# Attention rows: the copy of the attended values moves ahead of the second image's bias on VectorE

## What is computed

```python
x = x + _L0_conv_ref(_gn(x), ...)   # outlook attention: 3 x 3 patches weighted by a softmax over 9, 6 heads
x = x + _L1_conv_ref(_gn(x), ...)   # shifted-window attention: 7 x 7 windows, 12 heads of 16 channels
```

```python
attn = jnp.einsum('wmqd,wmkd->wmqk', q * hd ** (-0.5), k) + rpb[None]   # scores and relative bias
...
attn = jax.nn.softmax(attn.reshape(b * nW, NH, n, n), axis=-1)          # after the shift mask
out = jnp.einsum('wmqk,wmkd->wqmd', attn, v).reshape(b * nW, n, c)      # attended values
out = out @ proj_weight.T + proj_bias
```

## Time and profile before

| what | before |
|---|---|
| median of 3 runs | 3550.34 us (3539.38 to 3553.98) |
| profiled execution, own time | 3556.17 us |
| its span | 3554.1 us |
| TensorE busy (matmul) | 3286.0 us, 92% |
| VectorE busy | 2765.8 us, 78% |
| GpSimd busy | 2298.7 us, 65% |
| ScalarE busy | 1837.5 us, 52% |
| mean granted clock of TensorE | 0.957 |

### The profile page before, as it was taken

One profiled execution on the slowest core, in us unless ns is written; L12 is line 12 of the kernel. 1 busy time (PEld: TensorE's weight loads), 2 busy tenths in 40 slices (PEclk: granted clock), 3 DMA queues, 4 the chain that ended last, 5 costly groups with the idle time before them and its releaser, 6 DMA issues.

```text
span 3554.1 us, 105486 instructions
## 1 busy us (share of the span) xinstructions
PE 3286.0 (92%) x39908; PEld 1962.5 (55%) x39908; DVE 2765.8 (78%) x4561; ACT 1837.5 (52%) x3506; POOL 2298.7 (65%) x1889
## 2 busy tenths in 40 slices
PE   6989989899898998989989899898999989999998
PEld 3356644566445664456634666346663466634666
DVE  4968879678796887968879688796877878787786
ACT  3445644466444664456543556435654356544565
POOL 2867747677485774767647576476765667566674
PEclk7999999999999999999999999999999999999999
DMA  4732337322372323713246122561225612165122
GB/s 105 137 90 65 87 75 142 74 64 83 87 137 65 86 79 82 145 45 87 79 95 131 48 84 79 107 128 51 80 70 115 126 57 86 59 129 111 51 87 64
DMA packets 204335, 317.44 MB, mean 89 GB/s; under 512 B 16922, under 2 KB 176154, under 8 KB 203802
## 3 DMA queue, kind: packets, MB, share of 16 engines
q0 software_dynamic: 31936, 148.66, 21.5%
q1 hardware_dynamic: 171866, 161.61, 15.8%
HBM read 45.97 MB, written 38.54 MB: 24 GB/s over the span
## 4 chain that ended last, share of the span: by engine, by line
issue 28%; POOL 27%; PE 26%; DVE 8%; DMA 5%; ACT 4%; POOLq 1%; DVEq 0%; ACTq 0%; SPq 0%
POOL sp__70 L1796 11%; POOL sp__70 L1789 8%; DMA prod<-prod 5%; PE P L488 4%; DVE prod L1429 4%; POOL xr L1782 3%; POOL xw L1775 2%; PE P L393 1%; PE P L390 1%; POOL psum_p L1725 1%; PE P L493 1%; PE P L720 1%; PE P L506 1%; PE P L360 1%; PE P L409 1%
## 5 line engine op out<-in xcount | busy, mean ns | idle before, releaser
L1796 POOL TENSOR_TENSOR sp__70<-sp__70,rc 128x588 f32<-128x588 f32 x512 | 599.6, 1172 | 471.3 <-DVE rc L1558 458.0
L1429 DVE TENSOR_TENSOR prod<-P,vpad 128x896 f32<-128x896 f32 (+1 forms) x768 | 791.8, 1052 | 132.7 <-PE P L488 120.8
L1789 POOL TENSOR_TENSOR sp__70<-sp__70,mx 128x588 f32<-128x588 f32 x512 | 600.2, 1172 | 205.0 <-DVE mx L1548 204.8
L1124 ACT ACTIVATE sp__70<-sp__70 128x588 f32<-128x588 f32 x512 | 356.2, 697 | 586.9 <-POOL sp__70 L1789 586.8
L1555 DVE TENSOR_REDUCE sm<-sp__70 128x12 f32<-128x588 f32 x512 | 390.0, 762 | 305.8 <-ACT sp__70 L1124 305.5
L1541 DVE TENSOR_TENSOR sp__70<-P,relb 128x588 f32<-128x588 f32 x512 | 390.0, 762 | 158.8 <-PE P L720 150.2
L488 PE MATMUL P<-at,sel 108*128 108x448 bf16 x1512 | 427.4, 361 | 61.4 <-DVE prod L1429 31.0
L1709 POOL DMA_DIRECT2D prod<-prod x216 | 202.5, 941 | 368.0 <-DVE prod L1429 364.4
L1548 DVE TENSOR_REDUCE mx<-sp__70 128x12 f32<-128x588 f32 x512 | 389.8, 761 | 9.3
L733 PE MATMUL P<-ident,sp__70 113*98 113x113 f32 x3072 | 353.9, 267 | 18.9 <-DVE sp__70 L1541 18.9
L733 PEld LDWEIGHTS P<-ident,sp__70 113*98 113x98 f32 x3072 | 324.3, 131 | 79.7 <-issue 54.7
(11 more groups left out here) (257 smaller groups left out, 7170.6 us busy)
## 6 DMA issues: line engine op xcount, KB each, us to landing
prod<-prod POOLq DMA_DIRECT2D x216, 672.0 KB, 5.5
vbd<-vs SPq DMA_DIRECT2D x512, 147.0 KB
xin<-in_x SPq DMA_DIRECT2D x126, 336.0 KB, 5.2
out<-ot SPq DMA_DIRECT2D x184, 168.0 KB, 4.4
out<-ot SPq DMA_DIRECT2D x80, 84.0 KB
wn<-in_L_conv_qkv_weight SPq DMA_DIRECT2D x2, 432.0 KB, 6.7
wno<-in_L_conv_proj_weight SPq DMA_DIRECT2D x2, 144.0 KB, 7.2
self<-in_sel SPq DMA_DIRECT2D x3, 91.1 KB
```

Source lines behind the costliest of these rows:

```text
L1124: go(sp_[:, b, :], sp_[:, b, :], ACT.Exp).then_inc(p_exp, 1)
L1429: tt(by_row(dst), by_row(P[:, b:b + len(op), 0:CT]), val, ALU.mult).then_inc(prod_ok, 1)
L1789: tt(per_head(sp_[:, b, :]), per_head(sp_[:, b, :]), spread(mx[:, b, :]), ALU.subtract).then_inc(t_sub, 1)
L1796: tt(per_head(sp_[:, b, :]), per_head(sp_[:, b, :]), spread(rc[:, b, :]), ALU.mult).then_inc(p_norm, 1)
```

## The change

Inside `ahead`, the copy `keep_y(w, p)` moves from behind the second image's bias to directly behind the first image's bias. The first maximum, the second bias and the second maximum follow it in their old order. Nothing else is touched; the last row's turns that are written out by themselves keep their order.

```diff
@@ -1583,10 +1583,10 @@
                     w2, p2 = pair_after(w, p, AHEAD)
                     if w2 < NW:
                         score_bias(w2, p2, 0)
+                    keep_y(w, p)
+                    if w2 < NW:
                         score_max(w2, p2, 0)
                         score_bias(w2, p2, 1)
-                    keep_y(w, p)
-                    if w2 < NW:
                         score_max(w2, p2, 1)
```

## The result

| | before | after |
|---|---|---|
| median, 4 runs each | 3546.60 us (3539.38 to 3553.98) | 3580.36 us (3575.46 to 3586.14) |
| profiled execution | 3556.17 us, span 3554.1 | 3575.46 us, span 3573.4 |
| TensorE busy (matmul) | 3286.0 us | 3287.8 us |
| VectorE busy | 2765.8 us | 2767.1 us |
| mean granted clock of TensorE | 0.957 | 0.957 |

The ratio after to before is 1.0086, with a 95% interval of 1.0054 to 1.0118: the change costs about 30 us (19 to 42). The forecast was 25.6 us, or 3575.9 us with a range of 3554 to 3592. No engine does more work: the busy times of TensorE and VectorE agree within 2 us, GpSimd's is the same, and ScalarE's is 8 us less (1829.6 against 1837.5). So the time is in waits.

The account below looks back on a forecast made before the run. TensorE bounds the middle rows, with a slackless chain from the first maximum to it. Terms 16.4 + 3.2 + 1.9 + 3.5 + 0.6 = 25.6 us slower, from 3550.3 to 3575.9 us, range 3554 to 3592.

Parts of the forecast that it names:

- The 42 turns: p = 2 of rows 1 to 6: the first maximum's 0.39 us delay reaches TensorE whole through subtraction, exponential and `vs`; 16.4 us.
- The covered turns: p = 0, 1 and 3 of middle rows: delays of 0.24 to 0.47 us hidden by 0.8 to 1.35 us of cover.
- Row 1 with its pause: Six other row-1 turns where TensorE pauses inside the attended values, holding VectorE: 0.65 us in five of them, 3.2 us.
- (0,2): Row 0, p = 2: TensorE already waits for the second bias, so the 0.24 us delay costs at once; 1.9 us.
- (6,3): Row 6, p = 3: transposes wait for the second bias, scores for ScalarE behind the delayed exponential; 0.44 us each, 3.5 us.
- (7,0): Row 7, p = 0: statistics behind the second maximum slip 0.05 to 0.47 us, mostly covered; 0.6 us.
- Nothing earlier helps: `yt` is ready some 1.3 us sooner but no listed wait is for it: gain 0, at most 15.6 us.
- Given back at the wait for the keys: TensorE's 0.38 us key wait at p = 1 of middle rows shrinks by the stall; 9.6 us slower, 3560; chance 0.20.
- The earlier copy releases TensorE: TensorE gains at most the 15.6 us at L764's weight loads, stalls mostly absorbed; 3535 to 3541; chance 0.05.
- The copy holds VectorE longer than its pitch: The maximum waits for the copy's end, 0.11 us more in some 64 places; 7 us, 3583; chance 0.07.
- The clock falls at the longer stalls: Longer stalls before L695 lower TensorE's clock, slowing transposes in all 48 turns; 42 us more, 3618; chance 0.03.

Follow-up runs that it names:

- only_p2: Kernel before with the copy early only in the 48 turns p = 2 of rows 1 to 6; 3574.24 us, ratio 1.0061.
- covered: Kernel before with the copy early in 160 turns, not in p = 2 of rows 0 to 6, row 6 p = 3 or row 7 p = 0; 3560.38 us, ratio 1.0017.
- edge: Kernel before with the copy early only in row 6, p = 3 and row 7, p = 0, 16 turns in all; 3561.33 us, ratio 1.0027.
- mid_copy: Kernel before with the copy between the first maximum and the second bias, in all 232 turns; 3556.62 us, ratio 1.0015.
- vs_first_late: Kernel before with ScalarE's first window-value copies ahead of the p = 2 exponential in rows 1 to 6, and keep_y behind the second maximum; 3538.87 us, ratio 0.9957.
- copy_twice: Kernel after with the copy made twice in p = 2 of rows 1 to 6; 3598.00 us, ratio 1.0130 to the kernel before.
- only_70: Kernel before with the copy early only in row 7, p = 0; one profiled execution, 3564.15 us.

## Why the prediction was right

- **The 42 turns, 16.4 us.** Right in mechanism and in size: 0.39 us late at the maximum, 0.39 at L695, 0.39 to 0.40 in the row period. In the table (1,3) to (6,3) grew by 14.6 us for 40 rows (15.6 forecast), in only_p2 by 18.0.
- **The covered turns, nothing.** Right for rows 2 to 6. At p = 3 the first maximum is some 0.5 us late there, more than the 0.47 that the prediction had as the most, and is covered all the same. Wrong for row 1, as covered shows: 0.25 us a pair. In the kernel after, most of that hides behind the delay of p = 2: its pairs without a pause take 22.72 to 22.73 us from (1,0) to (1,3), 0.48 more than before, where 0.39 was forecast.
- **Row 1 with its pause.** The step was right in the turns where a pause occurred. In the third pair of after, with the bias at 1164.73, TensorE's timeline and VectorE's have these:
```profile
1166.77 0.23 PE L756 MATMUL P<-pt,vbd 98*32 98x49 f32 x1 [1.46 <-issue]
...
1167.04 0.47 DVE L1563 COPY yt<-P 128x294 f32<-128x294 f32 x1 [1.59 <-PE P L756]
...
1171.08 0.40 PE L695 MATMUL P<-wt,xw 64*98 64x192 f32 x1 [0.57 <-ACT vs L1117]
```
  From the copy to L695 it is 4.04 us, and the prediction's sum has 733.62 - 729.57 = 4.05. But the number of such turns was taken from one trace and isn't a property of the kernel: 6 pairs in that of before, 2 in that of after. That this term fitted into a right sum is luck.
- **(0,2), 1.9 us.** 119.6 - 117.5 = 2.1 us, though the kernels with an unchanged order there scatter from 116.2 to 117.5; the wait before the transposes is 1.99 us in all 8 pairs, where it was 1.77 to 1.79.
- **(6,3), 3.5 us, and (7,0), 0.6 us: mis-sized terms.** Together 6.9 us in the traces of after and of edge. At (6,3) the copy woke 0.11 us behind the modelled end of L756, not 0.04 (1330.03 + 0.78 = 1330.81, copy at 1330.92), so that the maximum was 0.51 late and not 0.44; the stretch grew by 4.3 us. At (7,0) the sum holds where L756 runs at full clock: the first maximum is 0.31 late in these four pairs of after, and the stretch takes 9.60 to 9.76 us. The step that failed is "mostly covered" where the clock is low. What a late maximum has beyond about 0.25 us comes out at the next bias, and with L756 at 1.22 us it is 0.77 late, where 0.47 was the bound. In the trace of after L756 lasts 1.22 us in four of the 8 pairs, and the stretch takes 10.06 or 10.07 us there; together 2.6 us more than before. The prediction also reasoned from the second maximum there.
- **Nothing earlier helps.** The 15.6 us of possible gain were 0: one wait of 0.5 us names `yt` as what ends last, and copies placed later than in the kernel after (mid_copy, vs_first_late) showed no new wait of TensorE for `yt`.

The rivals:
1. *Given back at the wait for the keys*: falls. That wait went from 34.1 to 32.8 us, the row period took the whole 0.39, and copy_twice another 0.52.
2. *The earlier copy releases TensorE*: falls, as above.
3. *The copy holds VectorE longer than its pitch*: falls. The pitch is 0.38 us also where the copy waited (1228.98 to 1229.36, and 463.71 to 464.09 behind a wait of 0.42). The Trainium skill ("VectorE: DVE Perf Modes", The DRAIN you can't avoid) would have it at 0.64 as an estimate. The prediction left out what the same section adds, that an operation which is not held starts earlier; the 0.38 measured agrees with that, and not with 0.64, for this pair of instructions. A real wait does cost 0.07 us more at (6,3) than the wake-up that I had read.
4. *The clock falls at the longer stalls*: falls for the middle rows, 1.00 with stalls of 0.6 us. The Trainium skill's warning of small idle times ("TensorE: Matmul & The Clock Gate", A second HAM failure mode: psum-queue depth-cycling) is not borne out there. The clock came in by another door: it was low at (7,0) already, in four pairs each of before and after, and the change made VectorE wait for TensorE just there.

**The sum against the times.** The profiled execution of after is 19.3 us longer than that of before. The row-1 pauses were worth 4.7 us more in the trace of before (7.8 us in six of them, 3.1 in two, over a mean pair without one), so like with like it is about 24 us, where the forecast has 25.6. The five narrow columns alone grow by 22.7 us, or 27.4 with the pauses taken out; what is outside them scatters. The ratio of the times gives 30, with 19 to 42 as interval. All agree with the sum; whether there are a few us more that no trace shows stays open.

## What to carry to other kernels

When an instruction that waits is moved ahead of others on an in-order engine, ask who waits for each instruction now queued behind it, and find for each turn the slack of that chain: here the 160 turns called covered cost 2 us in the trace, all of it in row 1, and 48 with no cover made some 70% of the loss. The listed idle time in front of a matmul can be less than what removing its wait gives (0.20 us listed, 0.31 gained in a middle row), and the place to look for gain is not the moved instruction but the engine in the middle of the chain: ScalarE's exponential stood ahead of a copy that TensorE needed sooner. Look at the clock and the duration of what is newly waited for in every stretch where it becomes a wait, not only in the middle rows.

## What the runs showed of the hardware that was not expected

- TensorE pauses of its own, with "issue" as reason: 1.31 us and 1.46 us before the last of 48 matmuls in row 1, in 6 of 8 pairs in one trace, 2 in another and none in that of covered. What makes them wasn't found out.
- A waiting copy starts 0.04 us behind the modelled end of its matmul in some turns and 0.11 in others, much the same from pair to pair at one place of the program (in the kernel after 0.04 at p = 2 of rows 2 to 6, 0.11 to 0.14 at (6,3)).
- The same 48 matmuls at the beginning of the last row take 1.22 or 1.23 us in four of 8 pairs of before and in four others of after, else 0.78 to 0.80. The longer duration goes with the lower granted clock in the table of only_70. From one pair to the next of one kernel the low stretch falls at different places; in only_70 it meets these matmuls whole in 7 pairs, in mid_copy in one. No run shows that the order on VectorE decides it.
- One execution of covered took 4476.76 us, where its other 11 took 3545.23 to 3565.84. It is left out of the comparison, and nothing explains it.
